# First experts: the low part of the up weights multiplied in two tiles of 64 rows

## The reference

```python
def _L0_ffn_ref(x, router_w, w1, w2, w3):
    ...
    flat = x.reshape(-1, C)
    logits = flat @ router_w.T
    probs = jax.nn.softmax(logits, axis=-1)
    topk_probs, topk_idx = jax.lax.top_k(probs, TOP_K)
    ...
    h1 = jnp.einsum('nc,ehc->neh', flat, w1)
    h3 = jnp.einsum('nc,ehc->neh', flat, w3)
    h = jax.nn.silu(h1) * h3
    y = jnp.einsum('neh,ech->nec', h, w2)
    out = jnp.einsum('ne,nec->nc', gates, y)
```

## Time and profile before

| | |
|---|---|
| median of 3 runs | 869.57 us (869.51 to 872.22) |
| the profiled execution | 870.85 us, span of the profile 868.4 us |
| PE / PEld busy | 633.8 us (73%) / 369.3 us (43%) |
| DVE / ACT / POOL busy | 557.7 us (64%) / 418.4 us (48%) / 247.3 us (28%) |

### The profile page before, as it was taken

One profiled execution on the slowest core, in us unless ns is written; L12 is line 12 of the kernel. 1 busy time (PEld: TensorE's weight loads), 2 busy tenths in 40 slices (PEclk: granted clock), 3 DMA queues, 4 the chain that ended last, 5 costly groups with the idle time before them and its releaser, 6 DMA issues. The chain is left out here.

```text
span 868.4 us, 8580 instructions
## 1 busy us (share of the span) xinstructions
PE 633.8 (73%) x2508; PEld 369.3 (43%) x2508; DVE 557.7 (64%) x1303; ACT 418.4 (48%) x667; POOL 247.3 (28%) x189
## 2 busy tenths in 40 slices
PE   4542989999947964769876579958687591887870
PEld 2441757777735823524443243434234430551120
DVE  1885566777745256487466486348455697769966
ACT  3002757888735313434565147113586350459930
POOL 5994457888741002010276050010000000000000
PEclk9999999999977995869955659759798655569985
DMA  3440000000014003020000030010000000000000
GB/s 100 121 121 0 2 0 1 2 0 1 2 29 72 0 6 132 1 76 0 1 2 1 0 75 1 1 58 1 15 1 2 16 0 0 2 0 0 0 0 12
DMA packets 18454, 18.47 MB, mean 21 GB/s; under 512 B 10947, under 2 KB 14340, under 8 KB 18025
## 3 DMA queue, kind: packets, MB, share of 16 engines
q1 hardware_dynamic: 18408, 17.94, 8.0%
HBM read 17.04 MB, written 0.26 MB: 20 GB/s over the span
## 5 line engine op out<-in xcount | busy, mean ns | idle before, releaser
L647 POOL TENSOR_TENSOR l0f_hid_lo<-l0f_hid,l0f_hid_hi 114x512 fp32r<-114x512 f32 (+1 forms) x75 | 98.1, 1317 | 55.0 <-ACT l0f_hid_hi L729 54.2
L825 DVE TENSOR_TENSOR l0f_hid<-l0f_silu,PS 114x512 f32<-114x512 f32 x96 | 65.7, 686 | 41.3 <-ACT l0f_silu L746 39.1
L683 PE MATMUL PS<-l0f_xs,l0w_hi 128*114 128x512 f32 x192 | 78.3, 408 | 0.0
L683 PE MATMUL PS<-l0f_xs,l0w_lo 128*114 128x512 f32 x192 | 77.4, 403 | 0.0
L746 ACT ACTIVATE l0f_silu<-PS 114x512 f32<-114x512 f32 x96 | 57.7, 601 | 31.1 <-PE PS L683 30.3
L2371 PE MATMUL PS<-l3f_ring,l3f_slots 128*32 128x512 f32 x128 | 54.6, 636 | 13.3 <-DVE l3f_ring L2481 13.3
L729 ACT CAST l0f_hid_hi<-l0f_hid 114x512 fp32r<-114x512 f32 x96 | 59.1, 615 | 2.4 <-DVE l0f_hid L825 1.8
L1303 POOL TENSOR_TENSOR l2c_den<-l2c_far,l2c_den 128x1024 f32<-128x1024 f32 x16 | 37.6, 2358 | 64.0 <-ACT l2c_den L1461 64.0
L2405 ACT ACTIVATE l3f_ring<-l3f_plain,l3f_neg 128x1024 f32<-128x1024 f32 x32 | 36.0, 1134 | 22.4 <-PE PS L2351 13.3
L2481 DVE SCALAR_TENSOR_TENSOR l3f_ring<-l3f_ring,l_countT 128x1024 f32<-128x1024 f32 x32 | 38.8, 1216 | 9.4 <-ACT l3f_ring L2409 9.4
L2456 DVE CUSTOM_DVE_ANT_0 l3f_ring<-l_count,l3f_srcw 128x1024 f32<-128x1024 f32 x32 | 39.2, 1225 | 5.8 <-ACT l3f_srcw L2393 4.8
(11 more groups left out here) (555 smaller groups left out, 1428.7 us busy)
## 6 DMA issues: line engine op xcount, KB each, us to landing
l0w_raw<-in_l_w SPq DMA_DIRECT2D x32, 170.5 KB, 3.2
l3k_edge<-in_edges SPq DMA_DIRECT2D x2, 1024.0 KB
l2c_wqkv<-in_l_wqkv SPq DMA_DIRECT2D x3, 384.0 KB, 4.2
l0w_w<-in_l_w SPq DMA_DIRECT2D x8, 142.5 KB
l2f_raw<-in_l_w SPq DMA_DIRECT2D x2, 512.0 KB, 6.5
l1c_pos_w<-in_l_pos_w SPq DMA_DIRECT2D x1, 784.0 KB, 5.2
l1c_vrow<-l1c_vimg SPq DMA_DIRECT2D x7, 88.0 KB, 3.7
l1f_raw<-in_l_w SPq DMA_DIRECT2D x2, 256.0 KB
```

Source lines behind the costliest of these rows:

```text
L647: g.tensor_tensor(hid_lo[0:k, q % HIDS, :], hid[0:k, q % HIDS, :], hid_hi[0:k, q % HIDS, :], ALU.subtract).then_inc(S("low_pool"), 1)
L683: last = t.matmul(m.PS[0:k, (one, two)[z], :], half[:, e, z, a:a + k], xs[:, h * HALF:(h + 1) * HALF], start=(half is ew.hi), stop=(half i ...
L825: v.tensor_tensor(hid[0:k, at % HIDS, :], silu[0:k, at % RING0, :], m.PS[0:k, two, :], ALU.mult).then_inc(S("free"), 1)
```

## The change

The two products with `hi` stay as they are. Of the products with `lo`, that of the first up weight contracts over partitions 0 to 63 only, and that of the second over partitions 64 to 127 only, each in a tile of 64 rows of the array (`tile_position`). A new tile `xr` holds the tokens' high part in partitions 64 to 127, where `xs` has the low part; ScalarE writes it with one more copy, and TensorE's first step waits for it. The product of the low part of the weights with the low part of the tokens, which the kernel before adds, is thereby left out. In the order within a step, both `hi` products now stand ahead of both `lo` products.

```diff
-        xs = sb("xs", [2 * C, T], F32R)
+        xs, xr = sb("xs", [2 * C, T], F32R), sb("xr", [2 * C, T], F32R)
...
                     if at == 0:
                         t.wait_ge(S("xs"), 2)
+                        t.wait_ge(S("xr"), 1)
...
                     a, k = HT[j]
+                    moving = slice(h * HALF, (h + 1) * HALF)
                     for z in range(2):
-                        for half in (ew.hi, ew.lo):
-                            last = t.matmul(m.PS[0:k, (one, two)[z], :], half[:, e, z, a:a + k], xs[:, h * HALF:(h + 1) * HALF],
-                                            start=(half is ew.hi), stop=(half is ew.lo))
+                        t.matmul(m.PS[0:k, (one, two)[z], :], ew.hi[:, e, z, a:a + k], xs[:, moving], start=True, stop=False)
+                    for z, x in enumerate((xs, xr)):
+                        rows = slice(z * C, (z + 1) * C)
+                        last = t.matmul(m.PS[0:k, (one, two)[z], :], ew.lo[rows, e, z, a:a + k], x[rows, moving],
+                                        start=False, stop=True, tile_position=(z * C, 0))
                 last.then_inc(S("up"), 1)
...
             a.copy(xs[0:C, :], m.XT[0:C, :]).then_inc(S("xs"), 1)
+            a.copy(xr[C:2 * C, :], m.XT[0:C, :]).then_inc(S("xr"), 1)
             a.wait_ge(m.sem("early_rw"), 32)
```

## The result

The changed kernel takes 884.18 us (median of 4 runs, 882.21 to 887.07), the kernel before 870.53 us in the runs beside it. The ratio is 1.0158, with a 95% interval from 1.0123 to 1.0193: it is slower by 13.7 us. 883.0 had been forecast.

What follows compares the result with a forecast made beforehand. The prediction took TensorE to bound the first experts' stage: 93 steps x 0.145 = 13.5 us, plus 0 for the copy, took the profiled 870.85 to 884.3, or 883.0 as a median; range of 8 in 10, 877 to 893.

Steps and rivals of the forecast that it cites:

- TensorE bounds the stage, and nothing hides a longer step: First experts: TensorE busy 120.00 of 120 us sets the pace; only the wait for the gate's transposes hides three steps.
- The step, +0.145 us: First experts' step: five slots of 0.233 plus 0.39 for leaving the full array and returning, 1.545 against 1.40 us.
- The intervals 0.33, 0.42, 0.34: TensorE starts: high product to low pair 0.32 to 0.33, then first down product 0.41 to 0.42, second 0.34 us.
- 93 steps, 13.5 us: First experts: 96 steps less three hidden in the wait for the gate's transposes, each paying 0.145: 13.5 us slower.
- The copy costs nothing: ScalarE's added copy of 0.95 us fits into 1.12 us idle before the exponential, free by 0.17.
- Serial halves: Rival: the low pair's halves run one after the other, two slots per step; +35 us, 905; chance 0.06.
- uncovered second load: Milder rival: the second half's weight load is uncovered too, 0.10 per step; +23 us, 892; chance 0.06.
- The fall of the clock: Rival: TensorE drops to 1.2 GHz in the first experts, at least 65 us more, above 935; chance 0.04.
- The rival on the other side: A pair costs no crossing: five slots, 1.167 a step, GpSimd needing 1.16; 848 to 851 us; chance 0.06.

Runs made afterwards that it cites:

- same_tile: Against the changed kernel, both low products run in the same tile, rows 0 to 63; 912.47 us, 1.0511 of the kernel before.
- two_trips: Against the changed kernel, order high, low, high, low, so the full array is left twice per step; median 1067.47 us (990.67 to 1085.56).
- five_slots: Against the changed kernel, one low product is left out and the other contracts over all 128 rows; 865.70 us, 0.9957 of the kernel before.
- four_slots: Against the changed kernel, both low products are left out, leaving four full matmuls per step; 866.52 us, 0.9959 of the kernel before.

## Why the prediction was right

**TensorE bounds the stage, and nothing hides a longer step.** Right: with the order and the copy alone nothing changed, and the whole loss is in the tiles.

**The step, +0.145 us.** Right in its sum and in its parts. From the first gate to the last up product, 75 steps, it was 109.9 us (129.3 to 239.2) and is 120.8: 0.145 per step. The intervals 0.33, 0.42, 0.34 are those named beforehand, the halves run at once, and the runs with twice and half the crossings put the step at 2.13 and 1.36, forecast 2.16 and 1.355. What a gate of 16 rows had shown held for tiles of 64 rows.

**93 steps, 13.5 us.** The sum fits the 13.7 measured, but not as the text had it, and that it fits so closely is partly luck. The stage lost 14.5 us in the profiles. The first 21 steps cost 3.6 instead of 2.6, since the clock rises 9.3 us later at the stage's start; the prediction had looked for a falling clock and not for a late rise. The prediction let the extra time of three steps vanish in the wait for the transposes. The wait did shrink, by 1.8 us, but mainly because TensorE came to it late from its slow start. An estimate by the lengths of a step at either clock (1.55 and 2.71 us changed, 1.40 and 2.56 before) closes the sum: 3.0 for all 21 steps, 4.0 for the late rise, less 1.6 for the stretch at 1.2 GHz behind the transposes, which fell away, and less 1.8 for the wait make 3.6. What lies outside the stage differed by 2.7 us between the two profiled executions, in the other direction, and hid it.

**The copy costs nothing.** Right, with less room than the 0.17 us claimed: it delays the exponential by about 0.08.

**The rivals.** Serial halves and an uncovered second load were excluded by the trace after and by same_tile. The fall of the clock did not happen in the change, but in two_trips, with twice the crossings. The rival on the other side was priced wrongly by a wide margin: the prediction added up GpSimd's 1.16 us of work per step and took that for the stage's next limit, but five slots give 1.45 per step with the gates (by the same count the kernel before has 1.465), and most of that gap goes away with VectorE's subtractions. By five_slots, even a free crossing would have ended near 866, not at 850.

## What to carry to other kernels

Row tiles pay only if a run of them is long enough to cover the way in and out: here a pair saves a slot of 0.23 us and the round trip costs 0.38, so one pair per excursion loses and two win. Before splitting a matmul, look in the trace for a place where the same engine already goes from the full array to a part of its rows, and read the two intervals on each side of it; "busy" does not show them. And before giving TensorE less to do, find what binds next by leaving its work out, not by adding up busy times: here 22 us less work bought 4.

## What the runs showed of the hardware

- Going from matmuls over the full array to ones in a part of its rows costs about 0.09 us until the next matmul starts, and about 0.10 for its weights, whose load starts with it and not ahead, each way, at 2.4 GHz. It made no difference whether the change was 128 to 64 rows, 128 to 16, or 16 to 64 (0.32 to 0.33 to the next start). The down products have 114 rows, and between them and those of 128 nothing is paid (0.23).
- Dense matmuls did not keep the clock up when each step crossed four times: it fell to 1.2 GHz at 262 us after 126 us at 2.4, with TensorE busy throughout, and stayed there for the 98 us to the last up product. With four slots, no crossing and TensorE idle 15% of the time it stayed up. With two crossings a step it stayed up too, but took 12.6 and 13.7 us to rise, and 36.1 with both low products in one tile; with four it took 43.8. What about a crossing counts for the clock is open. Without any, in four_slots, a rise took 8.8 us as well.
- Ahead of the trace's first entry on the clock the windows print 1.00, also where the intervals are those of 1.2 GHz (0.43 us for 512 columns; 93 to 128 us in same_tile).
- A subtraction of 114 x 512 on VectorE, 0.7 us at best, took up to 3.30 us beside three of GpSimd's.
